# Adding the mixture's gathered outputs to the residual: accumulating gathers in place of eight VectorE adds

## The chip, the cores and the metric

One core of one Trainium2 chip runs the kernel. The core has TensorE (PE in the profile) for matrix products, VectorE (DVE), ScalarE (ACT) and GpSimd (POOL) for the rest, SyncE (SP) that issues transfers, and 16 DMA engines that carry them. The engines run side by side and wait for each other on semaphores. PSUM holds what TensorE writes; SBUF is the working memory; HBM is the chip's main memory. The metric is the device time of one execution in microseconds, lower is better; three runs of the kernel before are shown with their median.

## What is computed

Two transformer layers over `x` of shape (8, 128, 128), that is 1024 rows (tokens) of 128 numbers. Each layer is cross attention to a context of 8 x 128 rows of 96 numbers, then a mixture of 8 experts. The layers differ: the first mixture sends a token to one expert only, the second weighs the two best. Cut to what matters:

```python
x = x + L0_xattn(layernorm(x), ctx)      # 16 heads of 8
x = x + L0_ffn(layernorm(x))             # one expert of 8 a token
x = x + L1_xattn(layernorm(x), ctx)
x = x + L1_ffn(layernorm(x))             # two experts of 8 a token

def L0_ffn(x):
    logits = einsum('btd,ed->bte', x, router_w)
    mask = one_hot(argmax(softmax(logits)), 8)
    h = square(relu(einsum('btd,edh->ebth', x, expert_fc)))
    out_e = einsum('ebth,edh->ebtd', h, expert_proj)
    return einsum('ebtd,bte->btd', out_e, mask)
```

The change is in the second line: how the result of `L0_ffn` gets into `x`.

## The kernel before

The residual `x` lies in SBUF as `xr`, 128 partitions x 8 batches x 128 numbers in fp32: one token a partition, one batch a block `xr[:, b, :]`. Everything else is written engine by engine: the order on each engine is the order of its block of code, and semaphores hold the engines together.

The first mixture is computed by sorting. VectorE works out for each token a slot in a table of 15 tiles of 128 slots, such that a tile holds tokens of one expert only (`slot_i`, one column a batch). GpSimd scatters the eight normalised blocks `xn[:, b, :]` into the HBM table `slots_x` at those slots, with eight indirect transfers (line 311). SP loads the table back as tiles, TensorE, ScalarE and VectorE put each tile through its expert, and SP stores each result tile into a second HBM table, `slots_y` (line 247). When all 15 stores have landed, GpSimd gathers: for each batch `b` one indirect transfer (line 317) brings, for each of the 128 partitions, the row of `slots_y` that its token's slot names. The target is `yg[:, b, :]`, a part of the buffer `work2` (printed as `work` in the profile, since buffer numbers are left out there). Each gather has a semaphore of its own, `gathered[b]`.

VectorE waits for gather `b` and adds it to the residual (line 671), four batches a half. Then come the statistics of the next layer norm for that half: `ln_stats` (lines 482, 485, 487: four BN_STATS, four BN_AGGR, one add of epsilon). GpSimd raises the variance to the power of minus one half (`rsqrt`, line 290). On GpSimd's queue the one of the first half, `rsqrt(2, 0)`, stands behind gather 5 and ahead of gathers 6 and 7; that of the second half stands behind gather 7. On VectorE's queue the normalisation of the first half (`ln_normalise(2, 0)`, line 496) stands behind the statistics of both halves. TensorE's next work is the transpose of the first normalised half (line 737), ScalarE copies it out (line 349), and the queries' projection for the second attention (line 744) follows. GpSimd then adds the output bias of that attention to `xr` (line 297), each half once it has been normalised.

Of the kernel before, what the change touches and what calls it, by code (L numbers as in the profile page):

```python
# [22 lines left out]
B, L, D = 8, 128, 128  # L23
# [41 lines left out]
def build(nc, x_in, ctx_in, wa_in, wr_in, fc_in, proj_in, w1_in, w2_in, b2_in, out):  # L65
    fp32, bf16, i32 = mybir.dt.float32, mybir.dt.bfloat16, mybir.dt.int32
    ALU, ACT, AX = mybir.AluOpType, mybir.ActivationFunctionType, mybir.AxisListType.X
# [3 lines left out]
    slots_y = nc.dram_tensor("slots_y", (TILES * P, D), fp32, kind="Internal").ap()  # L71

    ctx = ExitStack()
    with ctx:
        def sb(name, shape, dt=fp32):
            return ctx.enter_context(nc.sbuf_tensor(name, shape, dt))

        def sem(name):
            return ctx.enter_context(nc.semaphore(name))
# [24 lines left out]
        def wcol(layer, name):  # L104
            if layer == 0 and name in A_AT:
                lo, hi = A_AT[name]
                return wa[:, lo:hi]
            lo, hi = R_AT[name + str(layer) if name in ("wo", "bo") else name]
            return wr[:, lo:hi]


        xr = sb("xr", [P, B, D])
# [6 lines left out]
        work2 = sb("work2", [P, 2048])  # L119
# [30 lines left out]
        slot_i = sb("slot_i", [P, B], i32)  # L150
# [6 lines left out]
        hr = work[:, 3072:4096].rearrange("p (t f) -> p t f", t=2)  # L157
        h2 = work2[:, 0:1024].rearrange("p (t f) -> p t f", t=2)
        ys = sb("ys", [P, 2, D])
        yg = work2[:, 1024:2048].rearrange("p (b d) -> p b d", d=D)  # L160

        pr = sb("pr", [P, B, E])
        p2 = sb("p2", [P, B, E])
# [37 lines left out]
        gathered = [sem(f"gathered{b}") for b in range(B)]  # L201
# [60 lines left out]
        @block.gpsimd  # L262
        def _(pool):
            count = [0]

            def link(ins):
                count[0] += 1
                ins.then_inc(pool_chain, 1)
                pool.wait_ge(pool_chain, count[0])

            link(nc.gpsimd.memset(ones[:], 1.0))
            nc.gpsimd.affine_select(out=ident[:], in_=ones[:], pattern=[[-1, P]], compare_op=ALU.is_equal,
                                    fill=0.0, base=0, channel_multiplier=1).then_inc(pool_const, 1)
            nc.gpsimd.memset(minus_half[:], -0.5).then_inc(pool_const, 1)
            nc.gpsimd.memset(zeros[:], 0.0).then_inc(pool_const, 1)
            nc.gpsimd.iota(rank_down[:], pattern=[[-1, E]], base=E, channel_multiplier=0,
                           allow_small_or_imprecise_dtypes=True).then_inc(pool_const, 1)
            nc.gpsimd.iota(tile_no[:], pattern=[[1, TILES]], base=0, channel_multiplier=0,
                           allow_small_or_imprecise_dtypes=True).then_inc(pool_const, 1)
            link(nc.gpsimd.memset(upto[:], 1.0))  # L280
            nc.gpsimd.affine_select(out=upto[:], in_=upto[:], pattern=[[1, E], [-1, E]], compare_op=ALU.is_ge,
                                    fill=0.0, base=0, channel_multiplier=0).then_inc(pool_const, 1)
            link(nc.gpsimd.memset(ones_bf[:], 1.0))
            link(nc.gpsimd.affine_select(out=before[:], in_=ones_bf[:], pattern=[[1, P]], compare_op=ALU.is_gt,
                                         fill=0.0, base=0, channel_multiplier=-1))

            def rsqrt(k, half):
                pool.wait_ge(ln_var, 2 * k + half + 1)
                sl = slice(4 * half, 4 * half + 4)
                nc.gpsimd.tensor_tensor(rstd[:, sl], ve[:, sl], minus_half[:, sl], ALU.pow).then_inc(ln_rstd, 1)  # L290

            def add_bo(layer, k):
                pool.wait_ge(s_wr, 16)
                for half in range(2):
                    pool.wait_ge(ln_norm, 2 * k + half + 1)
                    sl = slice(4 * half, 4 * half + 4)
                    nc.gpsimd.tensor_tensor(xr[:, sl, :], xr[:, sl, :],
                                            wcol(layer, "bo").unsqueeze(1).to_broadcast([P, 4, D]),
                                            ALU.add).then_inc(bo_added, 1)

            rsqrt(0, 0)
            rsqrt(0, 1)
            add_bo(0, 0)
            rsqrt(1, 0)
            rsqrt(1, 1)

            pool.wait_ge(slot_rdy, 1)
            pool.wait_ge(s_zero, 16)
            pool.wait_ge(ln_norm, 4)
            for b in range(B):  # L310
                pool.indirect_dma_start(slots_x, bass.IndirectOffsetOnAxis(slot_i[:, b:b + 1], 0),  # L311
                                        xn[:, b, :], None).then_inc(scattered, 16)

            pool.wait_ge(y_out[0], 16 * ((TILES + 1) // 2))
            pool.wait_ge(y_out[1], 16 * (TILES // 2))
            for b in range(B):
                pool.indirect_dma_start(yg[:, b, :], None, slots_y,
                                        bass.IndirectOffsetOnAxis(slot_i[:, b:b + 1], 0)).then_inc(gathered[b], 16)
                if b == 5:
                    rsqrt(2, 0)  # L320
            rsqrt(2, 1)
            add_bo(1, 2)
            for j in range(4 * B):
                if j == 4 * B - 4:
                    rsqrt(3, 0)
                pool.wait_ge(p_exp, SB(1, j))
                nc.gpsimd.tensor_scalar(PT[:, j % PTR, :], PT[:, j % PTR, :], 1.0, FLOOR, ALU.min, ALU.max).then_inc(p_clamp, 1)  # L327
            rsqrt(3, 1)
# [140 lines left out]
        def _(dve):  # L469
            count = [0]  # L470

            def link(ins):

                count[0] += 1
                ins.then_inc(dve_chain, 1)
                dve.wait_ge(dve_chain, count[0])

            def ln_stats(k, half):
                bs = range(4 * half, 4 * half + 4)
                sl = slice(4 * half, 4 * half + 4)  # L480
                for b in bs:
                    ins = nc.vector.bn_stats(stats[:, b, :], xr[:, b, :])
                link(ins)
                for b in bs:
                    ins = nc.vector.bn_aggr(mv[:, b, :], stats[:, b, :])
                link(ins)
                nc.vector.tensor_scalar(ve[:, sl], mv[:, sl, 1], LN_EPS, None, ALU.add).then_inc(ln_var, 1)  # L487
# [179 lines left out]
            for half in range(2):  # L667

                for b in range(4 * half, 4 * half + 4):
                    dve.wait_ge(gathered[b], 16)  # L670
                    ins = nc.vector.tensor_tensor(xr[:, b, :], xr[:, b, :], yg[:, b, :], ALU.add)
                link(ins)
                ln_stats(2, half)
            ln_normalise(2, 0)
            ln_normalise(2, 1)
# [20 lines left out]
            ins = nc.vector.tensor_tensor(gates[:], gates[:], gsum[:].unsqueeze(2).to_broadcast([P, B, E]), ALU.mult)  # L696
            ins.then_inc(gates_rdy, 1)
            dve.wait_ge(gates_rdy, 1)
            for e in range(E):
                for half in range(2):  # L700
# [3 lines left out]
                    for i in range(4):  # L704
                        b = 4 * half + i
                        ins = nc.vector.scalar_tensor_tensor(xr[:, b, :], ps[:, 4 + half, 128 * i:128 * i + 128],  # L706
                                                             gates[:, b, e:e + 1], xr[:, b, :], ALU.mult, ALU.add)
# [11 lines left out]
        def _(pe):  # L719
# [231 lines left out]
            def xs_transpose(t):  # L951
                for i, (lo, _) in enumerate(XS_PARTS):
                    if t == lo:
                        pe.wait_ge(xs_in[i], 16)
                if t >= 1:
                    pe.wait_ge(xsT_sb, t)
                nc.tensor.transpose(ps[:, 2, 0:P], xs[:, t, :], ident[:]).then_inc(xsT_ps, 1)
# [157 lines left out]
```

## Time and profile before

| | us |
|---|---|
| median of the three runs | 298.69 |
| lowest and highest | 297.44 and 298.93 |
| the profiled execution, device time | 298.88 |
| its span, first to last instruction | 297.0 |

The profile gives for each engine the stretches in which it was busy, and for each idle stretch what ended it. Between the last result tile of the first mixture and the first transpose of the second attention the kernel goes through the gathers. A gather shows twice: as an instruction on POOL, which lasts while GpSimd writes the transfer's descriptors, and as a DMA, whose landing lets a waiting engine go on. A chain of waits is also given: for the work that ended last, what released it, and so on back to the start. The granted clock is that of TensorE, 1.00 being 2.4 GHz and 0.50 being 1.2 GHz.

### The profile page before, as it was taken

The page shows a single profiled execution, that of the slowest core. Times are in us where ns is not written, and L with a number is a line of the kernel's source. Part 1 is how long each engine was busy: PE and PEld are TensorE (multiplying, and loading weights), DVE is VectorE, ACT ScalarE, POOL GpSimd, SP SyncE. Part 2 cuts the span into 40 slices and gives each one's busy share as a digit, 9 for nine tenths or more (in the row PEclk, how much of TensorE's full clock was granted, in tenths as well). Part 3 has the DMA queues.
Part 4 walks back from the last instruction along what each step waited for, and adds up shares of the span by engine and source line. Part 5 has one row for each costly group of instructions (what it writes and reads, how often), then busy time and mean ns, then how long its engine had stood idle before and what let it go on. Part 6 is the DMA issues. An engine that isn't in the chain of part 4 may idle for free.

```text
span 297.0 us, 6196 instructions
## 1 busy us (share of the span) xinstructions
PE 235.6 (79%) x2411; PEld 172.1 (58%) x2411; DVE 141.4 (48%) x424; ACT 114.6 (39%) x218; POOL 50.3 (17%) x74
## 2 busy tenths in 40 slices
PE   0989889997467889995007897887965999999994
PEld 0347567775363479994003465665744577777774
DVE  5714467753623245552343355877544533332343
ACT  0544465554002736561002334545521444431440
POOL 2600000001105500000744003545531000000000
PEclk9999999999755979999555997999997699999999
DMA  7990000000000141101100000000000011110102
GB/s 253 407 399 34 3 3 4 7 4 2 0 0 27 49 130 35 40 27 38 44 27 1 0 4 4 3 6 5 3 2 0 0 35 39 35 35 2 44 27 71
DMA packets 12364, 13.73 MB, mean 46 GB/s; under 512 B 1224, under 2 KB 11344, under 8 KB 12080
## 3 DMA queue, kind: packets, MB, share of 16 engines
q1 hardware_dynamic: 10784, 11.77, 11.8%
q0 software_dynamic: 512, 1.05, 1.1%
q10 hardware_dynamic: 1040, 0.52, 0.7%
q8 instruction: 19, 0.31, 0.4%
q14 instruction: 9, 0.07, 0.1%
HBM read 10.19 MB, written 3.01 MB: 44 GB/s over the span
## 4 chain that ended last, share of the span: by engine, by line
PE 68%; DVE 10%; DMA 7%; issue 6%; POOL 5%; ACT 2%; POOLq 0%; SPq 0%; DVEq 0%; ACTq 0%
PE ps L808 11%; PE ps L1010 10%; PE ps L1019 10%; PE ps L744 6%; PE ps L965 5%; PE ps L847 4%; PE ps L975 4%; PE ps L816 4%; PE ps L724 4%; DVE mx L513 3%; POOL slots_x L311 2%; PE ps L859 2%; DMA wa<-in_wa 2%; DMA slots_y<-ys 2%; DMA work<-slots_y,slot_i 2%
## 5 line engine op out<-in xcount | busy, mean ns | idle before, releaser
L513 DVE TENSOR_REDUCE mx<-ps 128x4 f32<-128x512 f32 x64 | 41.3, 687 | 36.7 <-PE ps L808 36.6
L371 ACT ACTIVATE PT<-ps 128x512 f32<-128x512 f32 x64 | 35.7, 590 | 33.8 <-PE ps L816 33.8
L808 PE MATMUL ps<-k,q 32*128 32x128 f32 x512 | 38.1, 287 | 5.1 <-DVE mx L513 2.3
L808 PEld LDWEIGHTS ps<-k,q 32*128 32x128 f32 x512 | 32.2, 190 | 16.0 <-DVE mx L513 8.5
L816 PE MATMUL ps<-q,k 32*128 32x128 f32 x512 | 38.1, 288 | 0.0
L706 DVE SCALAR_TENSOR_TENSOR xr<-ps,gates,xr 128x128 f32<-128x128 f32 x64 | 18.0, 344 | 36.7 <-PE ps L1019 36.7
L1019 PEld LDWEIGHTS ps<-w,work 128*128 128x128 f32 x256 | 30.8, 192 | 6.4 <-issue 6.0
L462 ACT ACTIVATE work<-ps,w 128x512 f32<-128x512 f32 x32 | 21.8, 687 | 31.8 <-PE ps L1010 31.0
L816 PEld LDWEIGHTS ps<-q,k 32*128 32x128 f32 x512 | 31.9, 190 | 1.8 <-ACT PT L371 1.2
L1010 PE MATMUL ps<-xT,w 128*128 128x512 f32 x64 | 31.7, 623 | 0.0
L1019 PE MATMUL ps<-w,work 128*128 128x128 f32 x256 | 31.1, 275 | 0.0
L737 PE MATMUL ps<-ident,xn 128*128 128x128 f32 x32 | 6.9, 355 | 26.0 <-DVE xn L496 26.0
L327 POOL TENSOR_SCALAR PT<-PT 128x512 f32<-128x512 f32 x32 | 19.5, 620 | 37.9 <-ACT PT L371 37.9
L290 POOL TENSOR_TENSOR rstd<-ve,minus_half 128x4 f32<-128x4 f32 x8 | 8.3, 1033 | 82.3 <-DVE ve L487 82.3
L737 PEld LDWEIGHTS ps<-ident,xn 128*128 128x128 f32 x32 | 5.1, 185 | 28.1 <-issue 19.8
L349 ACT ACTIVATE xT<-ps 128x512 f32<-128x512 f32 x8 | 4.8, 596 | 42.3 <-PE ps L737 42.3
L847 PE MATMUL ps<-PT,vaug 128*32 128x128 f32 x512 | 21.1, 283 | 0.0
L355 ACT ACTIVATE k<-ps,bk 128x512 f32<-128x512 f32 x16 | 10.9, 687 | 17.2 <-PE ps L724 16.8
L975 PE MATMUL ps<-proj,work 128*128 x120 | 17.0, 285 | 0.7 <-DVE ys L652 0.6
L965 PE MATMUL ps<-xsT,work 128*128 128x128 f32 x120 | 17.4, 293 | 0.0
L661 DVE TENSOR_TENSOR work<-work 128x512 f32<-128x512 f32 x15 | 10.4, 692 | 14.7 <-ACT work L436 14.7
L1010 PEld LDWEIGHTS ps<-xT,w 128*128 128x128 f32 x64 | 11.7, 202 | 9.2 <-issue 9.2
(137 smaller groups left out, 313.7 us busy)
## 6 DMA issues: line engine op xcount, KB each, us to landing
proj<-in_proj SPq DMA_DIRECT2D x1, 2048.0 KB, 11.6
fc<-in_fc SPq DMA_DIRECT2D x1, 2048.0 KB, 17.9
w<-in_w SPq DMA_DIRECT2D x8, 129.0 KB, 2.1
w<-in_w SPq DMA_DIRECT2D x8, 128.0 KB, 2.2
q<-mT SPq DMA_DIRECT2D x64, 2.0 KB
slots_x<-zeros SPq DMA_DIRECT2D x1, 960.0 KB, 13.1
slots_y<-ys SPq DMA_DIRECT2D x15, 64.0 KB, 1.5
wr<-in_wr SPq DMA_DIRECT2D x1, 848.5 KB, 7.3
```

Source lines behind the costliest of these rows:

```text
L327: nc.gpsimd.tensor_scalar(PT[:, j % PTR, :], PT[:, j % PTR, :], 1.0, FLOOR, ALU.min, ALU.max).then_inc(p_clamp, 1)
L371: nc.scalar.activation(PT[:, j % PTR, :], ps[:, 3 + j % 3, :], ACT.Exp, scale=SCALE).then_inc(p_exp, 1)
L462: nc.scalar.activation(hT[:, half, c, :], ps[:, 2 * half + c, :], ACT.Gelu, bias=w1[:, e % 2, F1 + c:F1 + c + 1]).then_inc(hT_rdy, 1)
L513: nc.vector.tensor_reduce(mx[:, b, g:H:4], ps[:, j % 3, :].rearrange("p (k m) -> p k m", m=M), axis=AX, op=ALU.max).then_inc(s_top, 1)
L706: ins = nc.vector.scalar_tensor_tensor(xr[:, b, :], ps[:, 4 + half, 128 * i:128 * i + 128], gates[:, b, e:e + 1], xr[:, b, :], ALU.mult, A ...
L808: ins = mm(ps[:, (2 * n + i) % 3, P * k:P * k + P], q4[r:r + 32, k, L * b:L * b + L], k4[r:r + 32, k, M * b:M * b + M], start=True, stop=T ...
L816: ins = mm(ps[:, 3 + (2 * m + i) % 3, P * k:P * k + P], k4[r:r + 32, k, M * b:M * b + M], q4[r:r + 32, k, L * b:L * b + L], start=True, st ...
L847: ins = mm(ps[32 * k:32 * k + 32, 6, 128 * c:128 * c + 128], vaug[:, b, 4 * g + k, :], PT[:, j % PTR, 128 * k:128 * k + 128], start=first, ...
L965: ins = mm(ps[:, t % 2, P * c:P * c + P], fcb[:, t % 2, P * c:P * c + P], xsT[:, t % 2, :], start=True, stop=True)
L975: ins = mm(ps[:, 3, 0:D], h2[:, t % 2, P * c:P * c + P], proj[:, bass.ds(expert, 1), c, :].rearrange("p a d -> p (a d)"), start=(c == 0), ...
L1010: mm(ps[:, 2 * half + c, :], w1[:, e % 2, P * c:P * c + P], xT[:, 512 * half:512 * half + 512], start=True, stop=True).then_inc(up_ps, 1)
L1019: ins = mm(ps[:, 4 + half, P * i:P * i + P], hT[:, half, c, P * i:P * i + P], w2[:, e % 2, c, :], start=(c == 0), stop=(c == C1 - 1))
```

## The change

Each gather now accumulates: its target is `xr[:, b, :]` itself, and the transfer adds what it reads from `slots_y` to what stands there. The eight adds of VectorE are gone, with the buffer `yg` and the short wait behind the fourth add of a half. The waits for `gathered[b]` stay where they were, ahead of each half's statistics. The order of GpSimd's queue, the semaphores and all else stay.

```diff
-        yg = work2[:, 1024:2048].rearrange("p (b d) -> p b d", d=D)
...
             for b in range(B):
-                pool.indirect_dma_start(yg[:, b, :], None, slots_y,
-                                        bass.IndirectOffsetOnAxis(slot_i[:, b:b + 1], 0)).then_inc(gathered[b], 16)
+                pool.indirect_dma_start(xr[:, b, :], None, slots_y,
+                                        bass.IndirectOffsetOnAxis(slot_i[:, b:b + 1], 0),
+                                        compute_op=ALU.add).then_inc(gathered[b], 16)
                 if b == 5:
                     rsqrt(2, 0)
             rsqrt(2, 1)
...
                 for b in range(4 * half, 4 * half + 4):
                     dve.wait_ge(gathered[b], 16)
-                    ins = nc.vector.tensor_tensor(xr[:, b, :], xr[:, b, :], yg[:, b, :], ALU.add)
-                link(ins)
                 ln_stats(2, half)
```

On VectorE, between the copies of the last two result tiles and the normalisation, the instructions compare as follows (minus: only before, plus: only after; line 661 squares an expert's hidden layer, 652 copies a result tile out of PSUM):

```order
 L661 TENSOR_TENSOR work<-work 128x512
 L652 COPY ys<-ps 128x128 x2
-L671 TENSOR_TENSOR xr<-xr,work 128x128 x4
-L482 BN_STATS stats<-xr 128x6 x4
-L485 BN_AGGR mv<-stats 128x2 x4
-L487 TENSOR_SCALAR ve<-mv 128x4
-L671 TENSOR_TENSOR xr<-xr,work 128x128 x4
+L482 BN_STATS stats<-xr 128x6 x4
+L485 BN_AGGR mv<-stats 128x2 x4
+L487 TENSOR_SCALAR ve<-mv 128x4
 L482 BN_STATS stats<-xr 128x6 x4
 L485 BN_AGGR mv<-stats 128x2 x4
```

Only the two groups of four adds have gone; the two groups of statistics now stand directly behind each other and behind their waits.

On GpSimd the same stretch, from the end of the scatters to the clamps of the second attention, stood before as:

```order
L311 DMA slots_x<-xn,slot_i 1920x128 x8
L317 DMA work<-slots_y,slot_i 128x128 x6
L290 TENSOR_TENSOR rstd<-ve,minus_half 128x4
L317 DMA work<-slots_y,slot_i 128x128 x2
L290 TENSOR_TENSOR rstd<-ve,minus_half 128x4
L297 TENSOR_TENSOR xr<-xr,wr 128x512 x2
```

Now it reads (the new file's lines are one lower here):

```order
L310 DMA slots_x<-xn,slot_i 1920x128 x8
L316 DMA xr<-slots_y,slot_i 128x128 x6
L289 TENSOR_TENSOR rstd<-ve,minus_half 128x4
L316 DMA xr<-slots_y,slot_i 128x128 x2
L289 TENSOR_TENSOR rstd<-ve,minus_half 128x4
L296 TENSOR_TENSOR xr<-xr,wr 128x512 x2
```

Nothing has moved on GpSimd: the power of the first half still stands between the sixth and the seventh gather. Only the gathers' target differs.

## Rows read from the trace of the kernel before

**Rows 1.** The page: span, busy time by engine, and the chain's shares by engine.

```profile
span 297.0 us, 6196 instructions
...
PE 235.6 (79%) x2411; PEld 172.1 (58%) x2411; DVE 141.4 (48%) x424; ACT 114.6 (39%) x218; POOL 50.3 (17%) x74
...
PE 68%; DVE 10%; DMA 7%; issue 6%; POOL 5%; ACT 2%; POOLq 0%; SPq 0%; DVEq 0%; ACTq 0%
```

**Rows 2.** The chain that ended last, from 149.89 us: start, length, what.

```profile
149.89 0.19 issue
150.08 1.01 POOL work L317
151.10 0.30 issue
151.40 2.42 DMA work<-slots_y,slot_i
153.84 0.30 DVE xr L671
154.17 0.88 DVE stats L482 x4
...
155.57 1.13 DVE xn L496 x4
...
156.83 1.10 PE ps L737 x4
```

**Rows 3.** Instructions in order of time, 140 to 155 us: start, length, engine, line, operation.

```profile
140.55 0.98 POOL L317 DMA_INDIRECT work<-slots_y,slot_i  x1 [39.11 <-DMA slots_y<-ys]
...
144.43 1.00 POOL L317 DMA_INDIRECT work<-slots_y,slot_i  x1 [0.31 <-issue]
...
146.94 0.29 DVE L671 TENSOR_TENSOR xr<-xr,work 128x128 f32<-128x128 f32 x1 [1.01 <-DMA work<-slots_y,slot_i]
147.05 1.00 POOL L317 DMA_INDIRECT work<-slots_y,slot_i  x1 [0.30 <-issue]
147.27 0.87 DVE L482 BATCH_NORM_STATS2 stats<-xr 128x6 f32<-128x128 f32 x4
...
148.59 0.17 DVE L487 TENSOR_SCALAR ve<-mv 128x4 f32<-128x4 f32 x1
...
148.84 1.05 POOL L290 TENSOR_TENSOR rstd<-ve,minus_half 128x4 f32<-128x4 f32 x1 [0.79 <-DVE ve L487]
```

**Rows 4.** Line 317, the gathers: duration in ns (min/median/max), and time to landing.

```profile
L317 POOL DMA_INDIRECT work<-slots_y,slot_i x8: 954/1000/1027, 140.5 to 151.4; - x8
...
DMA to landing us min/median/max: 2.4/2.5/2.5
```

**Rows 5.** Line 311, the scatters, and line 247, the stores of result tiles, in the same view.

```profile
L311 POOL DMA_INDIRECT slots_x<-xn,slot_i x8: 954/958/1236, 91.4 to 100.5; - x8
...
L247 SPq DMA_DIRECT2D slots_y<-ys x15: 319/320/332, 111.2 to 138.8; - x15
...
DMA to landing us min/median/max: 1.5/1.5/3.4
```

**Rows 6.** Transfers from 141.8 to 143.2 us: DMA share and GB/s in 40 slices.

```profile
DMA  0000000000009979373000000000000000000000
GB/s 0 0 0 0 0 0 0 0 0 0 0 0 234 468 234 468 117 234 117 0 0 0 0 0 0 0 0 0 0 0 0 0 0 0 0 0 0 0 0 0
```

**Rows 7.** Busy time by stretch, instructions in brackets, then granted clock, DMA share, GB/s.

```profile
140.00:156.80 16.80, 0.00 (x0) 0.00 (x0) 6.11 (x30) 0.00 (x0) 10.07 (x10) 0.50 0.11 31
156.80:163.80 7.00, 6.28 (x10) 2.90 (x11) 1.91 (x4) 2.15 (x5) 2.20 (x3) 0.50 0.00 1
163.80:166.00 2.20, 1.24 (x5) 0.38 (x5) 0.00 (x0) 1.56 (x4) 0.00 (x0) 0.99 0.00 0
...
91.00:95.60 4.60, 4.49 (x6) 1.91 (x7) 0.69 (x4) 1.46 (x4) 3.32 (x4) 0.50 0.08 29
95.60:98.00 2.40, 2.40 (x7) 1.10 (x6) 0.00 (x0) 1.75 (x7) 1.79 (x3) 1.00 0.16 55
```

## The prediction, made before the changed kernel ran

> **What bounds the kernel now.** I read the page first [rows 1]. TensorE is busy 79% of the 297.0 us span and holds 68% of the chain that ended last, so most of the kernel is out of this change's reach. VectorE is busy 48% of the span, and its share of the chain is 10%. Taking 2.3 us of adds off an engine that is half idle is worth nothing in itself. What counts is only what lies on the chain.
>
> The chain in order of time [rows 2] says what does. From 149.89 to 156.83 us it runs GpSimd issuing gather 6 (1.01), gather 7 from issue to landing (2.42), one VectorE add (0.30), the four statistics, the normalisation of the first half, TensorE's transpose. In this stretch TensorE does nothing at all: from 140.0 to 156.8 us it has no instruction, at the lower granted clock of 0.50 [rows 7]. So every microsecond gained or lost between 140.55 and 156.83 goes straight into the time. Of the eight adds just one stands on this piece of the chain.
>
> The timeline [rows 3] gives the earlier part. The gathers are issued one after another, 1.00 us each with about 0.30 between them (140.55 for gather 0, 144.43 for gather 3). Gather 3 lands just before 146.94, when VectorE starts the fourth add. The statistics start at 147.27 and end at 148.59 + 0.17 = 148.76. GpSimd, which had finished issuing gather 5 at 147.05 + 1.00 = 148.05 and then sat idle for 0.79 us, starts the power for the first half at 148.84. Gathers 6 and 7 stand behind that power on GpSimd's queue. So the fourth add is on the path too, through GpSimd: what it delays, it delays for gathers 6 and 7. The other six adds are hidden: adds 0 to 2 finish while VectorE waits for the next gather, and adds 4 to 6 while it waits for gather 7.
>
> **The change, part by part.**
>
> Removed: the fourth add, 147.27 - 146.94 = 0.33 us from its start to the start of the statistics [rows 3]. The power can start 0.33 us earlier, since GpSimd has 0.79 us of idle time there to give. Removed too: the eighth add, 154.17 - 153.84 = 0.33 us [rows 2]. The six others give nothing. The gain is 2 x 0.33 = 0.66 us.
>
> Added: the accumulation. No transfer of the kernel before accumulates, so its price has to be bounded. It has two parts. Call x what an accumulating gather costs GpSimd more than a plain one to issue, and y what it takes more from the end of its issue to its landing. x enters many times, y twice:
> - gather 3 starts 3x later, is issued x later and lands y later: 4x + y. Less the 0.33 of the add, the power starts 4x + y - 0.33 later, as long as GpSimd is free by then. GpSimd is free 6x later (six gathers) less its 0.79 of idle time. The later of the two decides.
> - behind the power, gathers 6 and 7 add 2x, the landing adds y, and the add saved takes 0.33 away.
> - the sum, if VectorE's side decides: 6x + 2y - 0.66.
>
> The bounds of x. Below, zero: a scatter through the same indirect path takes 0.958 us at the median and a gather 1.000 [rows 4, 5], so the direction of the copy hardly matters, and with it perhaps not the kind. It could come out a little below: the fastest gather was issued in 0.954 [rows 4], and if the adds that run on VectorE beside the issues are what makes the median 1.000, taking them away gives 0.04 or 0.05 an issue, some 0.25 us over six. Above, 1.0 us: an accumulation has two operands to read, the row of the table and the row of the residual, and if GpSimd has to write a second set of descriptors for the second one, the 1.00 doubles. I take x = 0.3: the only indirect issue of the trace that departs from one microsecond is the first scatter at 1.236, which is 0.28 above its median [rows 5]; and a third kind of descriptor beside a read and a write would be half as much work again on the part of the 1.00 that goes by rows, which no row here separates from the fixed part.
>
> The bounds of y. The bytes of one gather pass in the slices 12 to 18 of 40 in a window of 1.4 us, that is 0.25 us [rows 6], while its landing comes 2.4 to 2.5 us behind the start of its issue [rows 4]: nearly all is latency. Below, zero: the second read runs beside the first and is hidden in that latency. Above, 1.5 us: the residual is read, added and written as a trip of its own, which costs what a store of the same 64 KB takes from issue to landing [rows 5]. I take y = 0.5: the bytes' 0.25 us once more, and as much again as a guess for rows that are added one by one and not passed on in one stream. It is nearer to the lower end because only 0.25 of the 2.5 us are movement of data.
>
> The sum with x = 0.3 and y = 0.5: the power starts 4 x 0.3 + 0.5 - 0.33 = 1.37 us later, at 150.21; GpSimd is free of gather 5 at 148.05 + 1.8 = 149.85, so VectorE's side decides. Gather 7 then lands 1.37 + 0.6 + 0.5 = 2.47 later, and the statistics start 2.14 us later than at 154.17. Normalisation, transpose and projection follow in the same order. 298.88 + 2.14 = 301.0 for the profiled execution; it stood 0.19 above the median of the runs, so the forecast for the median is 298.69 + 2.14 = **300.8 us**.
>
> A rule speaks for less. The trace shows a landing of 2.5 us for 64 KB [rows 4]. The Trainium skill, page "DMA: Bandwidth & Descriptors", section "Anatomy of one DMA — SWDGE (gpsimd) path", puts a transfer from GpSimd at about 2.0 us fixed plus its bytes at 436 GB/s, and says that many descriptors can be written before their cost shows. By that an estimate for the second operand's 64 KB is 0.15 us of y and nothing of x, and the sum would be 0.30 - 0.66 = -0.36 us.
>
> TensorE's clock also enters. It restarts at 156.83 and stays at 0.50 until about 163.8, some 7.0 us in which it is busy 6.28; elsewhere it restarted at 91.1 and got the full clock at 95.6, after 4.5 us [rows 7]. If the shift brings the restart to where the clock rises sooner, 2.5 us less are spent at half speed, worth up to 1.25 us; if it is worse placed, a few tenths are lost. I take nothing for it and keep -1.2 and +0.5 for the range.
>
> Hidden parts: the order on GpSimd and its waits are as before. The bias add of line 297, which writes the residual, stands behind all gathers, so nothing new waits there. SP has no transfer in this stretch. Behind it everything shifts as one block.
>
> **The rivals.**
>
> 1. The accumulation is nearly free (x and y small). For it: the plain transfers are nearly all fixed latency [rows 4, 6]. Against it: y counts twice and x six times, so x = 0.1 with y = 0.2 already turns the gain of 0.66 into a loss of 0.34. Price at x = y = 0: 298.69 - 0.66 = 298.0 us. This is the case that ends on the other side, not slower; it decides from 6x + 2y below 0.66 for a gain. To be over 0.5% faster it would need a help of the clock on top. For this rival speaks also the rule weighed above (the Trainium skill, page "DMA: Bandwidth & Descriptors"); by its estimate the time would be 298.3, and no row here shows an accumulation.
>
> 2. GpSimd becomes the bound: issuing an accumulating gather takes about twice as long (x = 1.0, y = 0.5). Then GpSimd is free of gather 5 only 6.0 - 0.79 = 5.21 us later, more than the 4.17 of VectorE's side, and the sum is 5.21 + 2.0 + 0.5 - 0.33 = 7.38: 306.1 us. For it: GpSimd writes the descriptors itself, at 1.00 us for 128 rows [rows 4]. Against it: the second operand needs no index and no table address.
>
> 3. The issue costs nothing and the landing much (x = 0, y = 1.5): each row is read, added and written in turn. The sum is 3.0 - 0.66 = 2.3: 301.0 us, in the same place as my forecast but for another reason; the durations on POOL tell them apart. The Trainium skill, same page, section "Rules for kernel authors", says that an accumulate reads its destination and writes it later, which is in favour of a y above zero.
>
> 4. The transfer doesn't do what it says, for instance the gathers are cut into smaller transfers with waits between them. Nothing in the order on GpSimd shows that; the price would be that of rival 2 or more.
>
> **How the numbers follow.** My forecast, with x between 0.2 and 0.5, or rival 3 with y above 1.1: 0.45 together, 0.37 of it for mine, 300 to 303 us. Rival 1 with its neighbours, up to 6x + 2y of 2.15: 0.33. Rival 2 and what lies between it and mine: 0.19. Rival 4: 0.03. What tells from no change here is about 0.5%, that is 1.5 us. Faster by more than that is only the clock's help on top of rival 1: 0.04. Within it is rival 1 and the lower edge of mine: 0.34. Slower: 0.62. The range runs from 297.8 (rival 1 with a little help of the clock) to 306.0 (just short of rival 2 at its full price), which leaves out about 2 in 10.
>
> **What would show it.** On POOL, the duration of an accumulating gather: 1.3 us by my forecast, 1.0 by rivals 1 and 3, 2.0 by rival 2. From the start of a gather's issue to its landing: 3.3 us by mine, 2.5 by rival 1, 4.0 by rival 3, 4.0 by rival 2. The idle time of POOL ahead of the first power: 0.36 us by mine (150.21 - 149.85), 0.46 by rival 1, none by rival 2. No add of line 671, and the statistics of the second half directly behind the landing of gather 7, at 156.3 us; TensorE's transposes start at 159.0. The prediction is wrong if a gather's issue is under 1.1 or over 1.6 us, or if the part behind 156.8 us doesn't keep its length to within the clock's 1.2.

## The result, and the profile after

| | before | changed |
|---|---|---|
| median of the first comparison, us | 298.06 (4 runs) | 303.38 (4 runs) |
| ratio, 95% interval | | 1.0175, 1.0128 to 1.0221 |
| median of a second comparison, us | 298.16 (17 runs) | 303.48 (6 runs) |
| ratio, 95% interval | | 1.0160, 1.0111 to 1.0208 |
| span of the profiled execution, us | 297.0 | 301.8 |

The changed kernel is slower by 1.6 to 1.75%, about 5 us. The forecast was 300.8 us with a range from 297.8 to 306.0. The ratio is estimated from all executions and isn't the quotient of the two medians, so a difference "in us" below, which is the ratio's share of the median before, can stand some tenths off the difference of the medians. Three executions of 472, 1214 and 528 us (two of the kernel whose last four gathers accumulate, one of the early normalisation) are in no ratio.

Line 316 of the changed kernel, the accumulating gathers, in the view of one line (duration in ns, min/median/max, and time from the start of the issue to the landing). It answers to [rows 4]:

```profile
L316 POOL DMA_INDIRECT xr<-slots_y,slot_i x8: 1534/1550/1622, 140.2 to 154.2; - x8
...
DMA to landing us min/median/max: 3.3/3.3/3.4
```

A gather keeps GpSimd for 1.55 us in place of 1.00 and lands 3.3 us behind the start of its issue in place of 2.5. So x, the extra at issue, is 0.55, and y, the extra from the end of the issue to the landing, is about 0.3.

The instructions in order of time, which answer to [rows 3]:

```profile
140.20 1.62 POOL L316 DMA_INDIRECT xr<-slots_y,slot_i  x1 [38.96 <-DMA slots_y<-ys]
...
149.38 0.87 DVE L482 BATCH_NORM_STATS2 stats<-xr 128x6 f32<-128x128 f32 x4 [10.98 <-DMA xr<-slots_y,slot_i]
149.52 1.54 POOL L316 DMA_INDIRECT xr<-slots_y,slot_i  x1 [0.30 <-issue]
...
150.70 0.17 DVE L487 TENSOR_SCALAR ve<-mv 128x4 f32<-128x4 f32 x1
150.96 1.19 POOL L289 TENSOR_TENSOR rstd<-ve,minus_half 128x4 f32<-128x4 f32 x1
```

The statistics end at 150.87, but gather 5 keeps GpSimd until 149.52 + 1.54 = 151.06. The row of the power has no idle time in brackets, where before it had 0.79 us: GpSimd, not VectorE, now says when the power runs. Its printed start, 150.96, lies inside gather 5's issue, and its 1.19 us are longer than the 1.05 of before; the chain below counts it from 151.06, and that start is used from here on. Its end, 152.15, is the same in both.

The chain that ended last shows the same (start, length, what), and answers to [rows 2]:

```profile
149.52 1.54 POOL xr L316
151.06 1.09 POOL rstd L289
...
152.33 1.60 POOL xr L316
...
154.24 3.26 DMA xr<-slots_y,slot_i
...
157.62 0.88 DVE stats L482 x4
...
159.03 1.13 DVE xn L496 x4
...
160.29 1.10 PE ps L735 x4
```

The chain no longer goes through VectorE ahead of the power: it runs from one POOL instruction to the next. It leaves GpSimd only with gather 7's transfer, whose landing VectorE waits for.

The two kernels' traces differ a little ahead of the gathers, so durations are best taken from the start of gather 0. From there, to:

| | before | changed | later by |
|---|---|---|---|
| the first power | 8.29 | 10.86 | 2.57 |
| gather 7's start | 10.85 | 14.04 | 3.19 |
| statistics of the second half | 13.62 | 17.42 | 3.80 |
| TensorE's restart | 16.28 | 20.09 | 3.81 |

In the second comparison's trace the last figure is 161.07 - 140.83 = 20.24, that is 3.96 later. From the restart to the end of the span it took 140.17 us before and 141.51 in the changed kernel (141.63 in its second trace). These 1.3 us (1.5 in the second trace) are not on the path of the gathers. Nearly all of them lie at the start of the second mixture, where the first eight products of line 1010 took 5.39 us and those of the changed kernel's line 1008, the same products, took 6.64. The timeline of TensorE, first of before and then of after:

```profile
232.06 5.39 PE L1010 MATMUL ps<-xT,w 128*128 128x512 f32 x8
```

```profile
235.58 6.64 PE L1008 MATMUL ps<-xT,w 128*128 128x512 f32 x8
```

The stretches of before, then of after, with the granted clock in the third place from the end:

```profile
232.00:235.50 3.50, 3.50 (x5) 1.55 (x6) 2.59 (x12) 1.55 (x3) 0.00 (x0) 0.50 0.00 0
235.50:237.30 1.80, 1.80 (x6) 0.78 (x5) 1.56 (x8) 1.80 (x3) 0.00 (x0) 1.00 0.00 0
```

```profile
235.60:240.60 5.00, 5.00 (x7) 2.14 (x8) 3.97 (x18) 2.81 (x4) 0.00 (x0) 0.50 0.00 0
240.60:242.20 1.60, 1.60 (x5) 0.67 (x4) 1.03 (x6) 0.69 (x1) 0.00 (x0) 0.71 0.00 0
```

Before, TensorE stayed at 1.2 GHz until 235.50, that is for 3.4 us of these products. After, the clock was still at 0.50 at 240.60, and the 0.71 of the next 1.6 us is a mean of 0.50 and 1.00: worked out from it, the clock rose at about 241.5, 5.9 us behind the start.

### The profile page after: what moved, and what is told of

Its sections match the earlier page's. It is cut to its first block, busy times and chain, and to the rows that moved or that the text cites. A ratio compares the mean times of both kernels' runs of the same rounds, so it can differ in the third digit from the quotient of the medians.

```text
span 301.8 us, 6192 instructions
## 1 busy us (share of the span) xinstructions
PE 235.9 (78%) x2411; PEld 172.3 (57%) x2411; DVE 139.3 (46%) x416; ACT 114.7 (38%) x218; POOL 55.0 (18%) x74
## 3 DMA queue, kind: packets, MB, share of 16 engines
q0 software_dynamic: 1408, 1.05, 2.0%
## 4 chain that ended last, share of the span: by engine, by line
PE 68%; DVE 10%; POOL 7%; issue 7%; DMA 5%; ACT 2%; POOLq 0%; SPq 0%; DVEq 0%; ACTq 0%
PE ps L806 11%; PE ps L1008 10%; PE ps L1017 10%; PE ps L742 6%; PE ps L963 5%; PE ps L973 5%; PE ps L845 4%; PE ps L814 4%; POOL xr L316 4%; PE ps L722 3%; DVE mx L513 3%; POOL slots_x L310 2%; DMA wa<-in_wa 2%; PE ps L857 2%; PE ps L869 1%
## 5 line engine op out<-in xcount | busy, mean ns | idle before, releaser
L1008 PE MATMUL ps<-xT,w 128*128 128x512 f32 x64 | 33.0, 645 | 0.0
L316 POOL DMA_INDIRECT xr<-slots_y,slot_i x8 | 12.5, 1565 | 41.0 <-DMA slots_y<-ys 39.0
```

Source lines behind the costliest of these rows:

```text
L316: pool.indirect_dma_start(xr[:, b, :], None, slots_y, bass.IndirectOffsetOnAxis(slot_i[:, b:b + 1], 0), compute_op=ALU.add).then_inc(gathe ...
L1008: mm(ps[:, 2 * half + c, :], w1[:, e % 2, P * c:P * c + P], xT[:, 512 * half:512 * half + 512], start=True, stop=True).then_inc(up_ps, 1)
```

## The experiments

The theory after the result: an accumulating gather costs GpSimd 0.55 us more and lands 0.3 us later behind that; eight of them fill GpSimd, and everything up to TensorE's restart follows by addition. The rivals: the price comes from taking the adds away or from their meeting with the gathers; or a mere shift of the gathers is what the rest of the kernel is paid for twice. A figure "from gather 0 to the restart" is the start of TensorE's first transpose less the start of gather 0 in the same trace. It is 16.28 before and 20.09 in the changed kernel (20.24 in its second trace). Gather 0 itself started anywhere from 138.4 to 141.0 us in traces with the same instructions ahead of it, which such a figure leaves out and a time doesn't.

### The adds alone

```diff
                     dve.wait_ge(gathered[b], 16)
-                    ins = nc.vector.tensor_tensor(xr[:, b, :], xr[:, b, :], yg[:, b, :], ALU.add)
-                link(ins)
```

> The kernel before with its plain gathers into the side buffer, and without the eight adds (the mixture's output is left out of the residual). The theory: only two of the eight adds stand on the path, 0.33 us each, so 298.1 - 0.7 = 297.4 us; on GpSimd a gather stays at 1.00 us and 2.5 us to landing, and the power for the first half starts 0.33 us earlier. The rival, by which the adds on VectorE also slow GpSimd's writing of descriptors: gathers at 0.95 us and 0.3 us more gain, 297.1 us. If the adds mattered little and something else in the changed kernel made it slow, this run would be slow too, about 300 us or more.

Measured: 296.98 us against 298.57, ratio 0.9969 (0.9938 to 1.0001), that is 0.9 us less, with an interval from 0 to 1.9. From gather 0 to the restart it took 154.30 - 138.44 = 15.86 us, 0.42 less than before. The fourth add gave 0.28 of it (the power starts 8.01 us behind gather 0 in place of 8.29); the eighth gave only 0.14 (from gather 7's start to the statistics 2.63 in place of 2.77). So all eight adds together, 2.3 us of VectorE's time, are worth half a microsecond to one, and the change could hardly have gained more than that. Its gathers took 0.94 to 1.01 us, 0.95 at the median, as the rival says by which the adds slow GpSimd. But the plain kernel with the late power, below, keeps all eight adds and has gathers of 0.94 to 0.99: the difference to the 1.00 of before doesn't come from the adds.

The adds put back behind accumulating gathers, with zeros in place of the gathered block:

```diff
                     dve.wait_ge(gathered[b], 16)
+                    ins = nc.vector.tensor_tensor(xr[:, b, :], xr[:, b, :], zeros[:], ALU.add)
+                link(ins)
```

> The accumulating gathers, and eight adds on VectorE at the old places, which add a block of zeros to the residual. The theory: a gather is issued in 1.55 us and lands 3.3 us from the start of its issue as in the changed kernel; with the add back the statistics of the first half end 0.33 us later and GpSimd, which is free of gather 5 some 0.2 us after them now, waits for VectorE again for 0.1 to 0.2 us; the eighth add costs 0.33 us. Together 0.5 us over the changed kernel: 303.9 us, and 5.8 over the kernel before. The rival, by which the accumulation's price comes from its meeting with VectorE's work on the same buffer: gathers over 1.6 us.

Measured: 302.75 us against 298.57, ratio 1.0157 (1.0114 to 1.0201). From gather 0 to the restart 159.79 - 139.45 = 20.34, 0.25 and 0.10 more than in the changed kernel's two traces; the timed runs can't tell the two kernels apart. I had expected 0.5. The fourth add is covered by gather 5's issue, as the trace shows: the power still has no idle time ahead of it, so at most the eighth add costs.

```profile
148.33 0.29 DVE L671 TENSOR_TENSOR xr<-xr,zeros 128x128 f32<-128x128 f32 x1 [1.41 <-DMA xr<-slots_y,slot_i]
148.65 0.87 DVE L482 BATCH_NORM_STATS2 stats<-xr 128x6 f32<-128x128 f32 x4
148.77 1.54 POOL L316 DMA_INDIRECT xr<-slots_y,slot_i  x1 [0.31 <-issue]
...
150.23 1.19 POOL L289 TENSOR_TENSOR rstd<-ve,minus_half 128x4 f32<-128x4 f32 x1
```

The gathers took the same 1.53 to 1.62 with the adds as without. The price is that of the accumulating gather, not of its company. No run gathers plainly into `xr`, so the kind of transfer isn't set apart from its target by a run of its own; the two targets have the same shape and row length.

### Half of the gathers

The first four accumulate, the last four are plain and keep their adds:

```diff
+                if b < 4:
+                    pool.indirect_dma_start(xr[:, b, :], None, slots_y,
+                                            bass.IndirectOffsetOnAxis(slot_i[:, b:b + 1], 0),
+                                            compute_op=ALU.add).then_inc(gathered[b], 16)
+                else:
+                    pool.indirect_dma_start(yg[:, b, :], None, slots_y,
...
+                    if not (b < 4):
+                        ins = nc.vector.tensor_tensor(xr[:, b, :], xr[:, b, :], yg[:, b, :], ALU.add)
```

> Gathers 0 to 3 accumulate and their adds are gone; gathers 4 to 7 are plain and are added on VectorE. With x = 0.55 us more to issue and y = 0.30 us more to land: gather 3 lands 4 x 0.55 + 0.30 = 2.50 us later, less the add 0.33, so the power starts 2.17 us later by VectorE's side; by GpSimd's side it would be 2.20 - 0.79 = 1.41. Gathers 6 and 7 are plain, so nothing is added behind it: 298.1 + 2.2 = 300.2 us. If only the occupancy of GpSimd mattered: 299.5 us. If the price came with gathers 6 and 7 alone: no change, 298 us.

Measured: 301.88 us against 298.57, ratio 1.0103 (1.0056 to 1.0150), 3.1 us with an interval from 1.7 to 4.5. From gather 0 to the restart 159.51 - 140.88 = 18.63, that is 2.35 more than before, against 2.17 worked out from x and y. The power waits for VectorE here, with the idle time that the kernel before had:

```profile
151.42 1.05 POOL L290 TENSOR_TENSOR rstd<-ve,minus_half 128x4 f32<-128x4 f32 x1 [0.79 <-DVE ve L492]
```

The mirror has the condition `b >= 4`.

> The mirror: gathers 0 to 3 are plain with their adds, gathers 4 to 7 accumulate. GpSimd's side: two longer issues ahead of the power, 1.10 - 0.79 = 0.31 us later; VectorE's side unchanged. Behind it gathers 6 and 7 add 2 x 0.55, the landing adds 0.30, the eighth add is gone (0.33): 0.31 + 1.10 + 0.30 - 0.33 = 1.38 us, 299.4 us. If only the landing counted (y twice, x hidden): 298.1 us or less.

Measured: the ratio is 1.0038 (1.0004 to 1.0072), 1.1 us, with an interval from 0.1 to 2.2. From gather 0 to the restart 158.63 - 140.97 = 17.66, that is 1.38 more than before, as expected. The median of the ten executions that count is 299.9 us against 298.87. The two halves together give 2.35 + 1.38 = 3.73, and the whole change 3.81 to 3.96. That they add up so well is in part luck: by the formula their sum is y - 0.33 more than the whole, and this happens to be near nothing.

### A mere shift

Three powers on four constants a partition, between the last store's landing and gather 0:

```diff
             pool.wait_ge(y_out[1], 16 * (TILES // 2))
+            for _ in range(3):
+                link(nc.gpsimd.tensor_tensor(filler[:], ones[:, 0:4], minus_half[:, 0:4], ALU.pow))
```

> The kernel before with three idle powers on GpSimd (4 numbers a partition each, some 1.1 us apiece) between the last store's landing and gather 0, so that everything from gather 0 on comes about 3.4 us later. It tells apart what the rest of the kernel does with a plain shift. The theory that a shift passes through unchanged: 298.1 + 3.4 = 301.5 us. The rival, that a longer idle stretch of TensorE is paid for again by a clock that rises later in what follows (as in the one profiled execution of the changed kernel, in which the part behind the first transpose took 1.3 us longer than before): 302.5 to 303.5 us.

Measured: 301.69 us against 298.57, ratio 1.0109 (1.0065 to 1.0152), 3.3 us with an interval from 1.9 to 4.5. The filler took from 139.14 to the start of gather 0:

```profile
139.14 3.21 POOL L318 TENSOR_TENSOR filler<-ones,minus_half 128x4 f32<-128x4 f32 x3 [38.07 <-DMA slots_y<-ys]
142.64 1.05 POOL L320 DMA_INDIRECT work<-slots_y,slot_i  x1 [0.29 <-POOL filler L318]
```

That is 3.50 us inserted and 3.3 paid: a shift passes through. From its restart at 159.02 to the end at 299.2 it took 140.2 us, as before. Its first products of the second mixture took 5.06 us, the shortest of all: the clock rose 2.7 us behind their start, at 237.3:

```profile
234.60 5.06 PE L1013 MATMUL ps<-xT,w 128*128 128x512 f32 x8
```

```profile
234.60:237.30 2.70, 2.70 (x4) 1.16 (x5) 1.95 (x9) 0.82 (x2) 0.00 (x0) 0.50 0.00 0
237.30:239.60 2.30, 2.30 (x7) 1.06 (x6) 1.99 (x10) 2.29 (x4) 0.00 (x0) 0.98 0.00 0
```

So a later start doesn't by itself cost clock. The changed kernel was run once more to see whether its 5 us hold:

> The changed kernel once more, unedited, in more rounds: the first measurement gave a ratio of 1.0175 with an interval from 1.0128 to 1.0221, that is 3.8 to 6.6 us. The trace puts 3.5 us of it ahead of TensorE's restart, and the plain shift by 3.5 us in the delayed kernel cost 3.3 us. If a shift passes through unchanged, the true difference is 3.5 to 4.5 us, 302.0 to 302.8 against 298.6. If the accumulation costs something that the stretch ahead of the restart doesn't show, it stays at 5 us or more.

Measured: 303.48 us against 298.16, ratio 1.0160 (1.0111 to 1.0208), 4.8 us with an interval from 3.3 to 6.2. The path accounts for 3.8 to 4.0 of it, which lies inside that interval. In its second trace, too, the first products of the second mixture took long, 6.69 us (line 1008). What I had taken from the delayed kernel, a difference of 3.5 to 4.5, is below both medians. About 3.9 us are shown on the path, and 1.3 to 1.5 us more show in both traces of the changed kernel behind the restart, with a later rise of the clock in the second mixture.

The traces of the other kernels tell against the accumulation as its cause. The same products were slow in the plain kernel with the late power (below), and fast in the kernel with accumulating gathers of three shapes (at the end of the experiments), where all eight accumulate. First the one and then the other:

```profile
229.94 6.48 PE L1010 MATMUL ps<-xT,w 128*128 128x512 f32 x8
```

```profile
234.36 5.27 PE L1015 MATMUL ps<-xT,w 128*128 128x512 f32 x8
```

From the restart to the end these two took 141.1 and 140.2 us. The early normalisation in the kernel before has the late rise too (6.29 us), and the late power in the changed kernel hasn't (5.43). So the rise moves between kernels with and without accumulation alike, and two traces of the changed kernel don't show that the extra belongs to the change. What sets it stays open.

### The place of the power

The power of the first half behind gather 7 in place of behind gather 5, in the kernel before:

```diff
-                if b == 5:
+                if b == 7:
                     rsqrt(2, 0)
```

> The kernel before with one thing moved: the power of the first half stands on GpSimd behind gather 7 in place of behind gather 5. Gather 6 no longer waits for the statistics: it starts at 148.05 + 0.30 = 148.35 in place of 150.08, so gather 7 lands 1.73 us earlier: 298.1 - 1.7 = 296.3 us. The power of the first half ends at about 151.7, before the statistics of the second half end at 153.8, so nothing waits for it. The rival, that GpSimd's queue isn't what holds gather 7: no change, 298 us.

Measured: 296.51 us against 298.87, ratio 0.9928 (0.9905 to 0.9951), 2.2 us less, with an interval from 1.5 to 2.8. From gather 0 to the restart 154.88 - 140.59 = 14.29, 1.99 less, where 1.73 was expected; the first six gathers were together 0.23 us shorter than in the trace of before (5.74 against 5.97), which is nearly all of the rest. On the path that is a bigger gain than all eight adds. It also confirms that gather 7's start was set by the power on GpSimd.

The same move in the changed kernel:

> The same move in the changed kernel. There GpSimd is already busy when the statistics end, so only the power itself goes from the path: gather 6 starts at 151.36 in place of 152.33, 1.0 us earlier: 302.4 us. Against the plain late-power kernel this is 8 x 0.55 + 0.30 - 0.33 = 4.4 us more, and a further us or so if a later start costs clock. If the wait for VectorE were still there, the gain would be the 1.7 us of the plain kernel.

Measured: 302.03 us against 298.87, ratio 1.0101 (1.0067 to 1.0134). From gather 0 to the restart 159.89 - 140.82 = 19.07, that is 1.02 less than the changed kernel's 20.09, as expected: only the power itself leaves the path, since GpSimd had no wait left to save. Against the plain kernel with the late power it is 4.78 more, where 4.4 was expected. With the power out of the way the accumulation costs more, because the idle time of GpSimd that had hidden 0.79 us of it is gone.

### TensorE no longer waits for the last gather

Both halves of the normalisation used to stand behind all statistics. The first half is moved ahead of the second half's waits, in the kernel before:

```diff
                 ln_stats(2, half)
-            ln_normalise(2, 0)
-            ln_normalise(2, 1)
+                ln_normalise(2, half)
```

> The kernel before with VectorE's normalisation of the first half moved ahead of the waits for gathers 4 to 7. The power of the first half ends at 149.89, so the first half is normalised by about 151.1 and TensorE transposes it and projects the queries of the first half (1.1 + 0.7 + 6.3 us) while gathers 6 and 7 are still on their way. TensorE restarts at 151.2 in place of 156.8; the scores of the second attention start some 5 us earlier, unless they wait for the second half: 293 to 294 us. The rival, that the later halves then hold the path and the gain comes back as waits: 296 us.

Measured: 294.05 us against 298.87, ratio 0.9820 (0.9783 to 0.9858), 5.4 us less. The medians lie 4.8 us apart. It is the fastest kernel of the study and beats both. Its timeline:

```profile
148.88 1.05 POOL L290 TENSOR_TENSOR rstd<-ve,minus_half 128x4 f32<-128x4 f32 x1 [0.99 <-DVE ve L487]
149.97 1.25 DVE L496 TENSOR_SCALAR xn<-xr,mv,rstd 128x128 f32<-128x128 f32 x4 [1.17 <-POOL rstd L290]
150.12 1.08 POOL L317 DMA_INDIRECT work<-slots_y,slot_i  x1 [0.19 <-issue]
...
151.36 1.09 PE L736 MATMUL ps<-ident,xn 128*128 128x128 f32 x4 [12.96 <-DVE xn L496]
```

TensorE restarts 10.82 us behind gather 0 in place of 16.28, while gathers 6 and 7 are still to come, and the projection of the queries hides them: the second half is normalised by 158.89, and TensorE transposes it at 160.51.

The same move in the changed kernel:

> The changed kernel with the normalisation of the first half moved ahead of the waits for gathers 4 to 7, as in the early-normalise kernel. There the restart of TensorE hangs on gather 3 and the power alone, no longer on gather 7. The power ends at 152.15 in place of 149.93, so TensorE restarts at 153.5 against 151.4: 2.1 us over the plain early-normalise kernel, 296.2 us. The second half is normalised at about 162.3, just ahead of where TensorE asks for it (162.9). The rival, that the second half becomes the wait: the full 3.5 us over the plain one, 297.6 us.

Measured: 295.99 us against 298.16, ratio 0.9933 (0.9907 to 0.9960). From gather 0 to the restart 152.17 - 138.79 = 13.38, 2.56 more than in the plain kernel with the same move; 2.1 was expected, since I took the restart from two traces whose gathers began 0.35 us apart. With the order mended, the accumulation still costs: the ratios of the two to their common kernel before are 0.9933 and 0.9820. It is cheaper than in the old order, as only gathers 0 to 5 are ahead of TensorE. The second half doesn't become the wait: it is normalised by 160.80, and TensorE transposes it at 161.75.

### What the price goes by

Gathers of three shapes, first plain and then accumulating; 4 and 5 have 64 partitions, 6 and 7 rows of 64 numbers:

```diff
+                if b in (4, 5):
+                    pool.indirect_dma_start(yg[0:64, b, :], None, slots_y,
+                                            bass.IndirectOffsetOnAxis(slot_i[0:64, b:b + 1], 0)).then_inc(gathered[b], 16)
+                elif b in (6, 7):
+                    pool.indirect_dma_start(yg[:, b, 0:64], None, slots_y.rearrange("r (h d) -> (r h) d", h=2),
+                                            bass.IndirectOffsetOnAxis(slot_i[:, b:b + 1], 0)).then_inc(gathered[b], 16)
...
```

> The kernel before without its adds (the mixture's output is left out of the residual), with plain gathers of three shapes: 0 to 3 are full, 4 and 5 have 64 partitions of 128 numbers, 6 and 7 have 128 partitions of 64 numbers. It is the measure for the next run. Expected on GpSimd: 0.95 us for the full ones and for the narrow rows, and between 0.5 and 0.8 us for the half-height ones, by what of the 0.95 goes by rows.

> The changed kernel with accumulating gathers of the same three shapes (half of gathers 4 to 7 is left out of the sum, and 6 and 7 add other rows). What the extra 0.60 us at issue (1.55 against 0.95) goes by: by rows, then 0.30 more than plain for the half-height gathers 4 and 5 and 0.60 more for the narrow 6 and 7; by bytes, then 0.30 more for all four; a fixed price of the kind of transfer, then 0.60 more for all four.

The plain ones, in the order half height, narrow, full:

```profile
L318 POOL DMA_INDIRECT work<-slots_y,slot_i x2: 907/910/912, 145.4 to 146.6; - x2
...
L321 POOL DMA_INDIRECT work<-slots_y,slot_i x2: 972/995/1018, 149.7 to 151.0; - x2
...
L324 POOL DMA_INDIRECT work<-slots_y,slot_i x4: 940/949/989, 140.4 to 144.2; - x4
```

The accumulating ones in the same order:

```profile
L317 POOL DMA_INDIRECT xr<-slots_y,slot_i x2: 1418/1424/1430, 146.8 to 148.5; - x2
...
DMA to landing us min/median/max: 2.9/2.9/2.9
...
L320 POOL DMA_INDIRECT xr<-slots_y,slot_i x2: 1576/1594/1613, 151.3 to 153.2; - x2
...
L323 POOL DMA_INDIRECT xr<-slots_y,slot_i x4: 1533/1550/1624, 139.3 to 145.0; - x4
```

Half the rows save 0.04 us of a plain issue (0.949 to 0.910) and 0.13 of an accumulating one (1.550 to 1.424). Half the bytes a row save nothing: gathers 6 and 7, narrow, took 1.02 and 0.97 plain, where the full ones of before took 1.01 and 0.97 in the same places. So the extra is 0.60 us for a full gather, 0.51 for half the rows and 0.60 for narrow ones: nearly a fixed price of the kind of transfer, with under 0.2 us that goes by 128 rows. None of the three pure cases I had set up fits exactly; the fixed one is the nearest. The landing's extra does shrink: behind the end of the issue a half-height gather lands at 2.9 - 1.42 = 1.5 us, as a plain one does (2.4 - 0.91), and so does a narrow one (3.1 - 1.59 against 2.5 - 1.00). Each kernel of shapes has one trace.

What the queue did is in the page, first of before and then of after (packets, MB, share of 16 engines, over all sixteen indirect transfers):

```profile
q0 software_dynamic: 512, 1.05, 1.1%
```

```profile
q0 software_dynamic: 1408, 1.05, 2.0%
```

The bytes are the same, and the eight gathers account for 896 more packets, 112 each. A plain transfer has 512 / 16 = 32, so an accumulating one has 144, if the scatters are as before. 112 more is what comes of 16 data packets cut into 128, one a row. The accumulating gathers of three shapes bear this out:

```profile
q0 software_dynamic: 1280, 0.92, 1.7%
```

One a row gives 6 x 112 more for the gathers of 128 rows and 2 x 48 for those of 64 rows: 768, and 1280 - 512 is 768.

## Why the prediction was right or wrong

**The view that only the path counts** was right. The eight adds alone, taken away, gave 0.4 us in the trace and 0.9 in the times, against 0.66 forecast; the fourth and the eighth were the ones on it, though the eighth gave 0.14 in place of 0.33.

**x** was mis-sized: 0.3 was taken, 0.55 against the median of before (and 0.60 against the shape test's plain 0.95) was measured. I had put it near the odd first scatter of 1.236, which has nothing to do with accumulation. The measured value lies between the bounds, 0 and 1.0. x counts six times in the forecast's sum and eight in the one that came true, so this is the term that made the forecast small. It also goes against my reason for it: I had split the 1.00 into a fixed part and one that goes by rows and expected the second to grow, whereas most of the extra is fixed.

**y** was taken as 0.5 and measured as about 0.3. With y twice in the forecast's sum that is 0.4 us too much, the other way. The landing 3.3 us behind the start of the issue came out just as forecast, and that is luck: x was 0.25 too small in it and y 0.2 too large.

**Which side decides** failed with x. At x = 0.3 VectorE's side set the power's start. At 0.55 GpSimd's does: 6 x 0.55 - 0.79 = 2.51 against 4 x 0.55 + 0.30 - 0.33 = 2.17, and 2.57 was measured. The 0.36 us of idle time forecast ahead of the power weren't there. The formula as written gives 2.51 + 1.10 + 0.30 - 0.33 = 3.58 with the measured terms; the trace has 3.81. The 0.23 missing is spread: 0.06 on the six issues ahead of the power, 0.04 around the power, 0.10 on gathers 6 and 7 (1.60 and 1.58 against 1.01 and 0.97) and 0.03 behind them. The structure of the second sum, GpSimd's side, therefore held, and rival 2's mechanism, GpSimd as the bound, came true with about half of its x. Of rival 4 one half came true: the transfer is cut finer, one packet a row, but the issues still stand 0.30 us apart, with no waits between.

**The clock** was taken as nothing with 0.5 us of allowance for the range. Both traces of the changed kernel show 1.3 to 1.5 us more behind the restart, over the 1.2 that the prediction named as a sign of being wrong, and not around the restart, where I had looked, but 75 us later, at the start of the second mixture. The delayed kernel shows none, a plain kernel (the late power) shows 1.0 and an accumulating one (the three shapes) none, so it isn't shown to come from the change.

**The sign and the range.** Slower by more than 0.5% was given 0.62 and is what happened, and the time lies in the range. That owes much to the range's width, which reached almost to rival 2 at its full price: the size was not right, 2.1 us forecast against 4.8 to 5.3. Of the 2.7 to 3.2 missing, 1.7 to 1.8 is the path (mostly x); the rest shows in the traces only as the late rise of the clock.

**The Trainium skill's fit**, page "DMA: Bandwidth & Descriptors", section "Anatomy of one DMA — SWDGE (gpsimd) path", would have given a gain of 0.36 us. For the plain gather its form holds to some 0.35 us, 2.5 measured at landing where about 2.15 comes out as an estimate. For an accumulating one the landing of 3.3 is well over it. That section calls the making of descriptors small. The measurement decides: the issue as a whole, of which the trace doesn't show the parts, keeps GpSimd for 1.55 us here, and it was the bound.

## What to carry to other kernels

Before moving arithmetic from an engine into a transfer, look at whether the arithmetic is on the path at all, and at who issues the transfer: here 2.3 us of adds, of which some half a microsecond counted, were bought with 0.55 us on each of eight issues, on the engine that the path went through. A cost that repeats in a queue has to be sized from the queue's side as well as from the waiting engine's side, because the one that decides can change with the size. And the cheap gain was next to it: letting TensorE start on the first half instead of waiting for both was worth about 5 us with one moved line.

## What the runs showed of the hardware that I had not expected

- An accumulating indirect gather of 128 rows of 512 bytes takes GpSimd 1.55 us against 0.95 to 1.00 for a plain one, and the extra is nearly fixed: 0.51 us with 64 rows, 0.60 with 128 rows of 256 bytes.
- It is cut into 144 packets in place of 32, and lands about 0.3 us later behind its issue; with 64 rows, or rows of half the bytes, there was no such lag.
- A plain gather of 64 rows is only 0.04 us shorter on GpSimd than one of 128, so of the shapes tried the large ones are the cheaper a byte.
- The place at which TensorE's clock rose in the second mixture moved between 2.7 and about 6 us behind the start of its products in kernels that run the same instructions there, and those products took from 5.06 to 6.69 us.
